# A graph network's layer-norm convolutions: node sums in a two-pair ring, normalised in place

## What is computed

```python
def _layernorm(x, axis=-1, eps=1e-05):
    m = jnp.mean(x, axis=axis, keepdims=True)
    v = jnp.var(x, axis=axis, keepdims=True)
    return (x - m) / jnp.sqrt(v + eps)
...
return x @ wself.T + eve @ weve.T + bias      # EVE convolution
...
return agg @ W_l.T + b + x @ W_r.T            # SAGE convolution
...
x = _layernorm(x + _L1_gnn_ref(x, src, dst, ...), axis=-1)
x = _layernorm(x + _L2_gnn_ref(x, edge_index, ...), axis=-1)
```

## Time and profile before

| | us |
|---|---|
| median of 3 runs | 10876.99 |
| lowest, highest | 10873.12, 10884.48 |
| the profiled execution, span | 15443.7 |
| of it stage m5 (8300 to 10050) | 1750 |
| of it stage m7 (11497 to 13215) | 1718 |

### The profile page before, as it was taken

One profiled execution on the slowest core, in us unless ns is written; L12 is line 12 of the kernel. 1 busy time (PEld: TensorE's weight loads), 2 busy tenths in 40 slices (PEclk: granted clock), 3 DMA queues, 4 the chain that ended last, 5 costly groups with the idle time before them and its releaser, 6 DMA issues. The chain is left out here.

```text
span 15443.7 us, 165743 instructions
## 1 busy us (share of the span) xinstructions
PE 7253.9 (47%) x36946; PEld 5501.8 (36%) x36947; DVE 6203.1 (40%) x16108; ACT 4646.1 (30%) x8631; POOL 7180.1 (46%) x7582
## 2 busy tenths in 40 slices
PE   1024544454534448854455555533334445445553
PEld 0024444444534444333333333323333333223332
DVE  3333433343434335522222333322223333378887
ACT  1111111111211114422222333412223333266676
POOL 4654444444454441144444444355554444557663
PEclk9987777777767779977777777866666667667776
DMA  6965554666656667644444444545555555233333
GB/s 164 209 154 171 172 167 148 205 200 194 202 176 198 193 194 255 235 142 158 143 166 143 162 160 159 177 144 173 168 171 170 183 177 192 81 104 119 114 114 100
DMA packets 1864962, 2570.76 MB, mean 166 GB/s; under 512 B 255901, under 2 KB 1369141, under 8 KB 1864662
## 3 DMA queue, kind: packets, MB, share of 16 engines
q1 hardware_dynamic: 1134168, 1627.20, 32.9%
q10 hardware_dynamic: 504726, 564.87, 11.2%
q0 software_dynamic: 225792, 375.94, 8.7%
HBM read 1499.55 MB, written 1129.98 MB: 170 GB/s over the span
## 5 line engine op out<-in xcount | busy, mean ns | idle before, releaser
L1078 POOL DMA_INDIRECT sums_gcn<-m_result,m_idx x1176 | 1162.8, 989 | 2311.9 <-DVE m_result L1399 1952.8
L1220 ACT ACTIVATE m_nodeT<-m_n_bank 128x512 f32<-128x512 f32 x980 | 544.3, 597 | 4220.6 <-remote 2400.8
L1626 PE MATMUL m_gram<-m_y 128*128 128x129 f32 (+1 forms) x4800 | 900.6, 336 | 1765.6 <-issue 1462.9
L1683 DVE SCALAR_TENSOR_TENSOR m_acc<-m_n_bank,m_scales,m_res_b 128x128 f32<-128x128 f32 (+1 forms) x2352 | 644.9, 343 | 2569.6 <-remote 1864.2
L1078 POOL DMA_INDIRECT sums_eve<-m_result,m_idx x784 | 762.7, 973 | 1696.8 <-DVE m_result L1515 1470.9
L1187 PE MATMUL m_n_bank<-k_ident,m_in_y 128*128 128x128 f32 x5488 | 895.6, 321 | 1310.0 <-DVE m_z L1772 826.9
L1772 DVE TENSOR_TENSOR m_z<-m_n_bank,m_in_sums 128x512 f32<-128x512 f32 (+1 forms) x784 | 511.9, 687 | 2412.8 <-remote 1300.2
L1626 PEld LDWEIGHTS m_gram<-m_y 128*128 128x128 f32 (+1 forms) x4800 | 801.2, 245 | 1845.4 <-issue 1523.6
L1078 POOL DMA_INDIRECT sums_sage<-m_result,m_idx x784 | 762.7, 973 | 1375.9 <-DVE m_result L1399 1134.3
L1070 POOL DMA_INDIRECT m_rows<-node_rows_a,m_idx x1176 | 1124.4, 956 | 358.5 <-issue 338.1
L1187 PEld LDWEIGHTS m_n_bank<-k_ident,m_in_y 128*128 128x128 f32 x5488 | 754.1, 168 | 1437.8 <-DVE m_z L1772 902.7
(11 more groups left out here) (302 smaller groups left out, 17415.1 us busy)
## 6 DMA issues: line engine op xcount, KB each, us to landing
m_in_sums<-sums_gcn SPq DMA_DIRECT2D x291, 512.0 KB
m_in_y<-node_rows_a SPq DMA_DIRECT2D x291, 512.0 KB
sums_gcn<-k_gcn_b SPq DMA_DIRECT2D x194, 512.0 KB
node_rows_a<-m_y ACTq DMA_DIRECT2D x194, 512.0 KB
m_in_x<-in_x_dram SPq DMA_DIRECT2D x194, 512.0 KB
m_in_y<-node_rows_b SPq DMA_DIRECT2D x194, 512.0 KB
sums_eve<-k_eve_b SPq DMA_DIRECT2D x194, 512.0 KB
m_in_sums<-sums_eve SPq DMA_DIRECT2D x194, 512.0 KB
```

The lines of the kernel that those rows point to most:

```text
L1078: pool.indirect_dma_start(self.node_sums[:, :], bass.IndirectOffsetOnAxis(self.idx[s][:, T + t:T + t + 1], 0), self.result[b][:, t, :], No ...
L1220: act.activation(out, src, ACT.Copy).then_inc(self.n_turn_read, 1)
L1626: mm = pe.matmul(self.gram[:, 0:D + 1], self.y1[b][0:rows[b], t, 0:D], self.y1[b][0:rows[b], t, :], start=False, stop=False, skip_group_ch ...
L1683: ins = dve.scalar_tensor_tensor(out=self.acc[b][0:n, tt, :], in0=ph.node_out(i, n)[:, t, :], scalar=self.scales[b][0:n, tt:tt + 1], in1=s ...
```

## The change

In the stages with a layer norm `z` and `o` are replaced by one tile `ring` of two pairs. Pair m lives in half m % 2. DVE adds into it, ACT normalises it in place, and the store goes out of it. DVE no longer waits for `finished`. The wait for the store (`out_free`, for both chunks) is taken from ACT's `finish_scalar` to DVE's `finish_vector`, ahead of `solve_scale`. Since m is a register in the loops, the half is chosen by an address from a register. The stages m4 and m6, whose finish is relu or swish, keep their code.

```diff
-        self.z, self.o = ([ph.sb(f"{n}{b}", [P, T, D]) for b in range(2)] for n in ("z", "o"))
...
+            self.ring = ph.sb("z", [P, 2, 2 * T, D])
...
+    def ring_of(self, m, b):
+
+        rows = slice(b * T, b * T + T)
+        if isinstance(m, int):
+            return self.ring[:, m % 2, rows, :]
+        return self.ring[:, bass.ds(m & 1, 1), rows, :].rearrange("p o t f -> p (o t) f")
...
-                dve.wait_ge(ph.finished, 2 * m + b + 1)
-            dve.tensor_tensor(self.z[b][0:n, half, :], ph.node_out(i, n), ph.buf["sums"][b][0:n, half, :], ALU.add).then_inc(ph.n_out_read, 1)
+                if not norm:
+                    dve.wait_ge(ph.finished, 2 * m + b + 1)
+                z = self.ring_of(m, b) if norm else self.z[b]
+            dve.tensor_tensor(z[0:n, half, :], ph.node_out(i, n), ph.buf["sums"][b][0:n, half, :], ALU.add).then_inc(ph.n_out_read, 1)
...
     def finish_vector(self, dve, m):
         if self.finish == "norm":
+            for b in range(2):
+                self.ph.out_free(dve, m, b)
             self.ln.solve_scale(dve, m)
...
+        past = m - 1 if isinstance(m, int) else m + 1
+        outs = []
         for b in range(2):
             n = ph.sh.rows((m - 1) * 2 + b)
-            ph.out_free(act, m, b)
             if self.finish == "norm":
-                self.ln.apply(act, self.o[b], self.z[b], n, b * T).then_inc(ph.finished, 1)
+                z = self.ring_of(past, b)
+                self.ln.apply(act, z, z, n, b * T).then_inc(ph.finished, 1)
+                outs.append(z)
...
-        ph.store_before(act, m, self.o)
+        ph.store_before(act, m, outs)
```

More of the change, by code:

```diff
@@ L1735, in __init__ @@
         self.ph, self.weight, self.finish = ph, weight, finish
-        self.z, self.o = ([ph.sb(f"{n}{b}", [P, T, D]) for b in range(2)] for n in ("z", "o"))
         self.z_done = ph.sem("z_done")
         if finish == "norm":
+            self.ring = ph.sb("z", [P, 2, 2 * T, D])
             self.ln = Norm(ph, "ln", 2 * T)
+        else:
+            self.z, self.o = ([ph.sb(f"{n}{b}", [P, T, D]) for b in range(2)] for n in ("z", "o"))
         self.grants = [(ph.nodes_turned, 2)] + [(ph.used[n], 2) for n in ph.used] + [(s, 16) for s in ph.stored]
@@ L1750, in tensor_end @@
         pass
+    def ring_of(self, m, b):
[3 more added lines that the diff above has]
+        return self.ring[:, bass.ds(m & 1, 1), rows, :].rearrange("p o t f -> p (o t) f")
     def vector_start(self, dve):
         for b in range(2):
-            dve.memset(self.z[b][:, :, :], 0.0).then_inc(self.z_done, 1)
+            z = self.ring_of(1, b) if self.finish == "norm" else self.z[b]
+            dve.memset(z[:, :, :], 0.0).then_inc(self.z_done, 1)
         if self.finish == "norm":
@@ L1776, in vector @@
                 if norm:
-                    ins = self.ln.take(dve, self.z[b], n, b * T)
+                    ins = self.ln.take(dve, z, n, b * T)
                 else:
@@ L1800, in finish_scalar @@
             act.wait_ge(self.ln.ready, m + 1)
+        past = m - 1 if isinstance(m, int) else m + 1
+        outs = []
         for b in range(2):
             n = ph.sh.rows((m - 1) * 2 + b)
-            ph.out_free(act, m, b)
             if self.finish == "norm":
-                self.ln.apply(act, self.o[b], self.z[b], n, b * T).then_inc(ph.finished, 1)
+                z = self.ring_of(past, b)
+                self.ln.apply(act, z, z, n, b * T).then_inc(ph.finished, 1)
+                outs.append(z)
             else:
+                ph.out_free(act, m, b)
                 act.wait_ge(self.z_done, 2 * m + b + 1)
                 act.activation(self.o[b][0:n, :, :], self.z[b][0:n, :, :], ACT.Relu if self.finish == "relu" else ACT.Silu).then_inc(ph.finished, 1)
-        ph.store_before(act, m, self.o)
+                outs.append(self.o[b])
+        ph.store_before(act, m, outs)
 def run_conv(nc, ph, edges, nodes):
```

## The result

The changed kernel takes 10995.54 us against 10880.74 for the kernel before, a ratio of 1.0103 (95% interval 1.0089 to 1.0117): 115 us slower. The forecast was 10943 us, and slower; the time lies just above the range.

What follows compares the result with a forecast made beforehand. The prediction took ACT's chain to bound m5 and POOL to cover m7. Its terms, +67 for the moved wait, -3 for m7's last step and +2 for addresses, gave +66 on 10876.99: 10943 us, own range 10900 to 10990.

Steps and rivals of the forecast that it cites:

- What bounds m5: In m5 ACT's chain of node and edge steps sets the pace, some 47 us a unit, above POOL's 40.5.
- DVE's earlier add is worth 0 in m5: In m5 DVE's add no longer waits for ACT's apply; claimed gain 0, since ACT's work follows on the chain.
- A steps: In m5, first of a unit's two successive node steps (B is the second); the moved wait costs nothing there.
- The price of the moved wait: In m5, waiting for both stores ahead of DVE's reciprocal costs 2.8 us in 24 steps: +67 us, bounds +29 and +94.
- L1 - L0: In m5, time between the landings of the first node step's two stores; taken as 2.2 us.
- worse than the sum: DVE's earlier adds let SP's transfers into the store's time: +48 us more, 10991; part of the 0.63 for slower.
- m7 at 0: In m7 the moved wait costs nothing and POOL's pace hides the earlier add's gain: 0, and -3 for the last step.
- Addresses at +2: On ACT and DVE the extra register-address instructions are hidden, except one after ACT's wait: +2 us in m5.
- POOL hides it: Rival: in a plain run m5 too goes at POOL's pace, so no change, 10877 us; chance 0.22.
- DVE's freedom counts: Rival: moved wait costs 0 to 29 us and m7's earlier adds gain 67: 10839, down to 10810; chance 0.15.

Runs made afterwards that it cites:

- the old code at plain pace: m5 as in the kernel before, profiled in the run with the ring in m7 alone; that run measured 1.0000 of the kernel before.

## Why the prediction was wrong

*What bounds m5*: right. The ring in m5 alone has all of the loss, and what apply stood longer (101 us) is nearly what m5 grew by (103.5); POOL did not cover it, and its waiting for results grew with it, from 178.8 us in the old code at plain pace to 285.1. The 47 us a unit, taken from the slow profile less its standstills, came out as 45.1 (1105.3 / 24.5) at plain pace, over POOL's 40.5.

*DVE's earlier add is worth 0 in m5*: right. It starts 3 us earlier in A steps, and no run shows a gain from it; what it does to SP's loads and the store counts against it, in the next item.

*The price of the moved wait*: this is the step that failed, by its size; the mechanism was right. The prediction took 2.2 us for L1 - L0 and 0.58 to apply, 2.8 a step and 67 us. The parts measured 2.9 and 0.7, and 4.2 together with what the ring adds: 101 us. The upper bound of 94 us was the nearer one, and it too fell short, because of two things. The gap L1 - L0 was estimated from single rows of a profile that ran 42% slow. There the last packet of A's two stores comes a median of 7.6 us after the issue, in the old code at plain pace 8.5; the later half is what the moved wait adds. The wait for the first half alone was not undersized: it is 2.0 us on average in both (46.6 / 23 and 53.2 / 27). That POOL's transfers, which lay apart from the burst in the earlier trace rows, run into it at plain pace would fit, but is not shown. And the store of after is not the store of before: with the ring the same wait is 0.6 us longer than its two parts, and the store's last packet 0.6 us later, with SP's second `sums` load issued ahead of it. I had this as a rival ("worse than the sum", up to 48 us) and left it out of the sum; some 15 us (101.0 - 68.5 - 17.1) of the loss are of that size.

*m7 at 0*: right in the sum, wrong in one reason. "The same wait costs nothing there, since the stores have longer" is not so: the reciprocal waited 219.6 us for stores in m7. POOL waited only twice for a result in m7, 19.9 us; that this cover hid both the wait and the gain of the earlier add is the reading that fits, and m7's length, 962.3 against 964.4 us, agrees.

*Addresses at +2*: near enough. After the shift, apply starts 0.70 us later instead of 0.62, and 16 activations take 6.28 us instead of 6.26; over 49 steps that is some 5 us.

*POOL hides it* fell with m5's growth, *DVE's freedom counts* with m7's 0. The Trainium skill, page "DMA: Bandwidth & Descriptors", section "Anatomy of one DMA — SWDGE (gpsimd) path", gave as an estimate some 4.4 us for two such stores. B's stores with 0.48 MB of SP's beside them, under 5 us, agree with that; A's, in a full stretch, took more than twice as long. The rule of the Trainium skill, same page, section "Issuing engines are not separate DMA queues", that all issuing engines' transfers interleave on the same 16 engines would fit the difference; no run here shows it apart. The Trainium skill, page "Perfetto Trace Analysis", section "Identifying the Most-Contended Engine", would have had POOL set the pace: in m7 it does, in m5 POOL waits 285.1 us for results.

## What to carry to other kernels

When a wait is moved to another engine, count what is queued behind it there: DVE did not need the store until its add, but the reciprocal that ACT's chain hangs on stood behind the wait, and merging two waits into one made the chain wait for the later store. A buffer that is saved (no output tiles, no wait of DVE for ACT) was worth nothing here on an engine with slack, and it let other transfers start ahead of the store that is waited for. Here the wait belonged right ahead of the first instruction that overwrites the buffer; there the same ring gained 17 us instead of losing 115.

## What was not expected of the hardware

The kernel before took 15443.7 us in its profiled execution, and twelve changed forms of it between 10862 and 11058 us in theirs, so waits sized in one profile should be held against the unprofiled time first. And a store's time from issue to landing went with what else was on the DMA engines: under 5 us with 0.48 MB beside it, more than 11 us in a stretch of share 0.95. Taking 1 MB of fills a pair away did not shorten it; the next loads came in their place. It also went with which engine issued first: with SP's second `sums` load ahead of the stores instead of behind them, their first packet came 3.9 us after the issue instead of 2.5.
